# Exchange of keys and outputs from SBUF to SBUF, and a reordered front and border, in a linear-attention and FP4 network kernel

## What is computed

```
xn = layernorm(x)
# attention block, H = 8 heads, DK = DV = 128, chunks of 128 tokens
h  = rmsnorm(xn) * attn_norm_w
q, k, v = h @ Wq, h @ Wk, h @ Wv                      # 256 -> 1024 each
per head, chunk after chunk, state S (128 x 128):
    o = tril(q k^T) v + q S ;  S = S + k^T v
o  = rmsnorm(o) * out_norm_w                          # per head
x2 = xn + o @ Wo
s  = x2 + (silu(h2 @ Wgate) * (h2 @ Wup)) @ Wdown     # h2 = rmsnorm(x2) * mlp_norm_w, 1024 wide
# second network on xn, activations and weights rounded to FP4 in blocks of 16
g  = silu(fp4_linear(silu(gate4) * up4, w_down))      # 704 wide
out = x + s * g
```

## Time and profile before

| | before |
|---|---|
| median of 3 runs | 1065.65 us (1065.02 to 1065.74) |
| the profiled execution | 1065.84 us, its span 1064.1 us |
| PE busy | 1052.4 us, 99% |
| DVE busy | 904.9 us, 85% |
| ACT busy | 526.8 us, 50% |
| granted TensorE clock | 1.00 |
| q1 (SP's DMAs) | 141.88 MB, 43.1% of 16 engines |

### The profile page before, as it was taken

One profiled execution on the slowest core, in us unless ns is written; L12 is line 12 of the kernel. 1 busy time (PEld: TensorE's weight loads), 2 busy tenths in 40 slices (PEclk: granted clock), 3 DMA queues, 4 the chain that ended last, 5 costly groups with the idle time before them and its releaser, 6 DMA issues.

```text
span 1064.1 us, 18735 instructions
## 1 busy us (share of the span) xinstructions
PE 1052.4 (99%) x6792; PEld 961.5 (90%) x6792; DVE 904.9 (85%) x1859; ACT 526.8 (50%) x1481; POOL 47.3 (4%) x68
## 2 busy tenths in 40 slices
PE   8999999999999999999999999999999999999998
PEld 6899999998999989999998889999999999999997
DVE  6788888888888888888887798888888889889887
ACT  6664655755656546557555634443333333243332
POOL 0000000000000000000000000101001010101010
PEclk9999999999999999999999999999999999999999
DMA  7455355455364553554545723253433233323213
GB/s 244 143 160 175 106 173 168 138 156 167 134 192 133 157 175 120 184 173 127 166 149 161 195 68 97 80 158 94 120 90 119 85 120 98 122 85 93 86 57 112
DMA packets 166219, 143.07 MB, mean 134 GB/s; under 512 B 28784, under 2 KB 162928, under 8 KB 166128
## 3 DMA queue, kind: packets, MB, share of 16 engines
q1 hardware_dynamic: 165440, 141.88, 43.1%
q10 hardware_dynamic: 688, 0.00, 0.0%
HBM read 77.27 MB, written 64.57 MB: 133 GB/s over the span
## 4 chain that ended last, share of the span: by engine, by line
PE 89%; DMA 4%; DVE 2%; SPq 2%; ACT 2%; issue 1%; POOL 0%; DVEq 0%; ACTq 0%; POOLq 0%
PE ps L261 69%; PE ps L712 5%; PE ps L756 5%; PE ps L750 4%; PE ps L736 4%; DMA moved<-work 3%; DMA r_gate<-moved 1%; SPq L410 1%; PE ps L838 1%; PE ps L639 1%; PE ps L599 1%; SPq L482 1%; DMA work<-kept_xq 1%; ACT work L945 0%; DVE work L1361 0%
## 5 line engine op out<-in xcount | busy, mean ns | idle before, releaser
L261 PE MATMUL ps<-r_k,r_gate_up 128*128 128x512 f32 x768 | 185.2, 391 | 0.5 <-DVE r_k L1544 0.5
L261 PEld LDWEIGHTS ps<-r_k,r_gate_up 128*128 128x128 f32 x768 | 141.5, 188 | 27.9 <-issue 0.7
L261 PE MATMUL ps<-r_o,onT 128*128 128x256 f32 x768 | 106.9, 288 | 0.4 <-DVE onT L1267 0.4
L261 PE MATMUL ps<-r_h,r_k 128*128 128x512 f32 (+1 forms) x393 | 105.2, 403 | 0.0
L261 PEld LDWEIGHTS ps<-r_q,r_v 128*128 128x128 f32 x768 | 99.7, 191 | 4.9 <-DVE r_v L1612 0.3
L261 PE MATMUL ps<-r_q,r_v 128*128 128x256 f32 x768 | 102.3, 283 | 0.0
L261 PE MATMUL ps<-r_h,r_q 128*128 128x512 f32 x384 | 98.1, 391 | 0.0
L945 ACT ACTIVATE work<-ps 128x128 f32<-128x128 f32 x256 | 67.1, 277 | 62.2 <-PE ps L756 62.1
L261 PE MATMUL ps<-r_v,r_h 128*128 128x512 f32 x384 | 97.4, 390 | 0.0
L261 PEld LDWEIGHTS ps<-r_o,onT 128*128 128x128 f32 x768 | 95.7, 190 | 0.8 <-DVE onT L1267 0.7
L921 ACT ACTIVATE work<-ps 128x512 f32<-128x512 f32 x64 | 38.3, 599 | 108.6 <-PE ps L261 108.6
(11 more groups left out here) (160 smaller groups left out, 1987.6 us busy)
## 6 DMA issues: line engine op xcount, KB each, us to landing
moved<-work SPq DMA_DIRECT2D x63, 512.0 KB, 2.9
r_gate<-moved SPq DMA_DIRECT2D x252, 128.0 KB, 2.5
kept_h<-work SPq DMA_DIRECT2D x31, 384.0 KB, 2.6
work<-kept_h SPq DMA_DIRECT2D x124, 96.0 KB, 2.3
work<-in_L_attn_hidden_states SPq DMA_DIRECT2D x15, 512.0 KB, 5.2
kept<-work SPq DMA_DIRECT2D x9, 514.0 KB, 4.3
kept_h<-work SPq DMA_DIRECT2D x9, 512.0 KB, 3.7
kept_xq<-work SPq DMA_DIRECT2D x8, 512.0 KB, 5.4
```

The lines of the kernel that those rows point to most:

```text
L261: done = pe.matmul(out_ap, a, b, start=first and n == 0, stop=last and n == 2, skip_group_check=skip)
```

## The change

- `exchange` has no tile in HBM. Four DMAs go from `leaving` to `arriving`, the q-th reading slot q of all 128 partitions and writing 32 partitions with four such slots each. They are issued when keys and outputs are ready in `leaving` and `arriving` has been read by both turns. `moved_out` is gone; who waited for it waits for `moved_in`, the landing of all four.
- A destination partition now holds four neighbouring source partitions and not four that are 32 apart, so both DVE turns write with "(d a)" in place of "(a d)": every fourth column of a row.
- ACT: `permute_k` comes before `copy_k` and both after one wait; the wait is for `moved_in`. PE's `turn_h` waits for `copy_k` in addition.
- DVE: `ln_roots` with `rms_factor` (h=1) and `x2_factor` (h=3) come before the turns and no longer behind them.
- Front: WARM 4 instead of 5; Wo is loaded after the first exchange, into another place, and split in two parts in steps 0 and 1 (ACT) and 1 and 2 (DVE); PE waits for weight parts 4, 5 and 6 each before its first use and not for all before step 0; ACT's order of weights and copies is changed; x of block 1 is loaded after the exchange.
- Border: the loads of `kept_xq` and `kept_w4` are issued in steps 11 and 12 of the last batch instead of both in 13; `xT_hi_of` on ACT comes in step 14 right behind `copy_k`; one product of the second network is put ahead of an output projection.

```diff
-                    sp.dma_start(moved.rearrange("b p x -> p b x"), leaving.rearrange("p b i x -> p b (i x)"))\
-                      .then_inc(moved_out, 16)
                     if again:
                         sp.wait_ge(k_tok_ready, value - 1)
                     if turned_o is not None:
                         sp.wait_ge(oT_ready, turned_o)
-                    sp.wait_ge(moved_out, 16 * value)
                     for q in range(QUADS):
-                        sp.dma_start(arriving[q * QUAD:(q + 1) * QUAD].rearrange("p a i x -> p a (i x)"),
-                                     moved[q].rearrange("(a p) x -> p a x", a=QUADS)).then_inc(moved_in, 16)
+                        sp.dma_start(arriving[q * QUAD:(q + 1) * QUAD].rearrange("p a i x -> p (a i x)"),
+                                     leaving[:, q, :, :].rearrange("p i x -> p (i x)")).then_inc(moved_in, 16)
...
-                    dve.transpose(k_tok.rearrange("p c (a d) -> p c a d", a=QUADS), k_landed).then_inc(k_tok_ready, 1)
+                    dve.transpose(k_tok.rearrange("p c (d a) -> p c a d", a=QUADS), k_landed).then_inc(k_tok_ready, 1)
...
-                    dve.transpose(oT.rearrange("p c (a d) -> p c a d", a=QUADS), o_landed).then_inc(oT_ready, 1)
+                    dve.transpose(oT.rearrange("p c (d a) -> p c a d", a=QUADS), o_landed).then_inc(oT_ready, 1)
...
-        WARM = 5
+        WARM = 4
...
-                for i, (n, c0, c1) in enumerate(w_parts):
...
+                for i in range(W_OUT):
+                    load_weight(i)
...
                 exchange(1, again=False)
+                sp.dma_start(raw_out, Wo.rearrange("(h p) n -> p h n", p=P)).then_inc(w_loaded[W_OUT], 16)
+                sp.wait_ge(xn_ready, 1)
+                sp.dma_start(x_in, x_blocks[1]).then_inc(x_loaded, 16)
...
-                pe.wait_ge(w_ready, W_OUT)
                 pe.wait_ge(q_ready, 1)
...
                         pe.wait_ge(k_perm_ready, t0 + j + 1)
+                        if (b, j) == (0, 0):
+                            pe.wait_ge(w_ready, 4)
                         project(wk, B_K, h_next, s_next, k_done)
+                        if (b, j) == (0, 0):
+                            pe.wait_ge(w_ready, 5)
                         project(wq, B_Q, h_next, s_next, q_done)
+                        if (b, j) == (0, 0):
+                            pe.wait_ge(w_ready, W_OUT)
...
                 weight_hi(2)
+                permute_k(1)
+                copy_k(1)
                 weight_hi(3)
-                copy_k(1)
-                permute_k()
-                for i in range(4, len(w_parts)):
-                    weight_hi(i)
                 copy_q(1, 0)
-                act.wait_ge(w_ready, 5)
-                for c in range(CH):
+                weight_hi(4)
+                act.wait_ge(w_ready, 4)
+                copy_v(1, 0, 0, FIRST_V_BANKS[0])
+                weight_hi(5)
+                for c in range(1, CH):
                     copy_v(c + 1, 0, c, FIRST_V_BANKS[c])
...
-                        copy_k(t0 + j + 2)
-                        if not (final and j == STEPS - LAG):
-                            act.wait_ge(moved_out, 16 * (t0 + j + 1))
-                            permute_k()
+                        if not (final and j == STEPS - LAG):
+                            act.wait_ge(moved_in, 16 * QUADS * (t0 + j + 1))
+                            permute_k(t0 + j + 2)
+                        copy_k(t0 + j + 2)
+                        if final and j == STEPS - LAG:
+                            xT_hi_of(0, range(KD))
...
+                    if first and j < 2:
+                        weight_out_hi(j)
...
+                    if n == 0 and h in (1, 2):
+                        weight_out_lo(h - 1)
...
+                    if h == 1 and ahead:
+                        ln_roots(1 - s, n + 1, mine)
+                        rms_factor(1 - s, mine)
+                    if h == 3:
+                        x2_factor(n + 1, mine)
                     if not (final and j == STEPS - 1):
                         turn_k(t0 + j + 1)
...
-                        dve.wait_ge(moved_out, 16 * (t0 + j + 2))
+                        dve.wait_ge(moved_in, 16 * QUADS * (t0 + j + 2))
...
                 gate_up4(0, 0, (0,), (1,))
+                gate_up4(0, 0, (1,), (0,))
                 out_projection(H - 2, batches * STEPS - 1)
-                gate_up4(0, 0, (1,))
+                gate_up4(0, 0, (1,), (1,))
```

More of the change, by code:

```diff
@@ L168, in build @@
         raw_w = [work[:, at:at + WCOLS].rearrange("p (k n) -> p k n", k=KD)
-                 for at in (v_at, v_at + WCOLS, not_yet)]
-        raw_w.append(work[:, not_yet + WCOLS:not_yet + 2 * WCOLS].rearrange("p (h n) -> p h n", h=H))
+                 for at in (v_at + WCOLS, v_at, not_yet)]
         stats = one.cut(CH, 6)
@@ L175, in build @@
         small = one.cut(12, CH)
+        out_at = one.at
         xq_new = one.cut(CH * D)
@@ L183, in build @@
         assert one.at - down4_at >= N4P and max(PIECE4) <= CH * D
+        assert one.at - out_at >= WCOLS
+        raw_out = work[:, out_at:out_at + WCOLS].rearrange("p (h n) -> p h n", h=H)
         leaving = one.cut(QUADS, 2, CH * QUAD)
@@ L278, in build @@
         FIRST = 2 * P
-        w_parts = [(1, 0, FIRST), (0, 0, FIRST), (2, 0, BANK), (1, FIRST, HD), (0, FIRST, HD), (2, BANK, HD), (3, 0, D)]
+        w_parts = [(1, 0, FIRST), (0, 0, FIRST), (2, 0, BANK), (1, FIRST, HD), (0, FIRST, HD), (2, BANK, HD)]
         W_OUT = 6
-        projections = ((Wq, wq), (Wk, wk), (Wv, wv), (Wo, wo))
-        w_loaded = [sem(f"weight_part{i}_loaded") for i in range(len(w_parts))]
+        projections = ((Wq, wq), (Wk, wk), (Wv, wv))
+        w_loaded = [sem(f"weight_part{i}_loaded") for i in range(len(w_parts) + 1)]
         w_hi, w_ready = sem("weight_hi_done"), sem("weight_ready")
@@ L456, in attention_transfers @@
                             sp.wait_ge(piece_ready, n)
+                        else:
+                            sp.wait_ge(w_ready, W_OUT + 2)
                         load_piece(n, range(QUADS // 2) if h == CH + 1 else range(QUADS // 2, QUADS))
@@ L760, in attend @@
                         if (j - LAG) % H == 0:
-                            pe.wait_ge(w_ready, len(w_parts))
                             pe.wait_ge(x2_summed, n0 + s + 1)
+                        if first and j - LAG in (0, CH):
+                            pe.wait_ge(w_ready, W_OUT + 1 + (j - LAG) // CH)
                         out_projection((j - LAG) % H, t0 + j - 1)
@@ L921, in copy_k, with permute_k @@
                     act.activation(kT, ps[:, B_K, :], ACT.Copy).then_inc(k_ready, 1)
-                def permute_k():
+                def permute_k(value):
+                    act.wait_ge(k_done, value)
                     act.activation(k_perm,
@@ L1009, in weight_hi, with weight_out_hi @@
                     act.wait_ge(w_loaded[i], 16)
-                    scale = nw_out[:, 0:1] if n == 3 else 1.0
-                    act.activation(projections[n][1][:, HI, :, c0:c1], raw_w[n][:, :, c0:c1], ACT.Copy, scale=scale)\
+                    act.activation(projections[n][1][:, HI, :, c0:c1], raw_w[n][:, :, c0:c1], ACT.Copy).then_inc(w_hi, 1)
+                def weight_out_hi(i):
+                    act.wait_ge(w_loaded[W_OUT], 16)
+                    heads = slice(i * CH, (i + 1) * CH)
+                    act.activation(wo[:, HI, heads, :], raw_out[:, heads, :], ACT.Copy, scale=nw_out[:, 0:1])\
                        .then_inc(w_hi, 1)
@@ L1086, in attention @@
                             weights4_hi(2 + k, raw_gate4[:, k, :])
-                        xT_hi_of(0, range(KD))
                     if final and last:
@@ L1372, in early_extras @@
                         fp4_grid(piece, grid_w, mine)
-                    if h == 1 and ahead:
-                        ln_roots(1 - s, n + 1, mine)
-                        rms_factor(1 - s, mine)
                     if h == 2 and n:
                         residual(1 - s, n)
-                    if h == 3:
-                        x2_factor(n + 1, mine)
                     if h == 3 and rounds_piece:
@@ L1498, in attention @@
                             turn_o()
-                    if first and j == 0:
-                        weight_lo(W_OUT)
-                        dve.wait_ge(w_ready, len(w_parts))
                     early_extras(b, j, mine)
```

36 lines of the change are left out of this document (19 added, 17 removed).

## The result

The changed kernel takes 1083.44 us (median of 4 runs, 1082.53 to 1084.62) beside 1065.7 for the kernel before (4 runs, 1065.02 to 1066.6): a ratio of 1.0166, 95% interval 1.0153 to 1.0178. It is 17.7 us slower where 8.3 us faster was forecast, and outside the range. The mechanism is that of rival A, at about two thirds of the price that it gave a turn (the rows are 0.38 to 0.40 us longer, not 0.57). The profiled execution took 1083.64 us, its span 1081.9, at a granted clock of 1.00 as before.

A forecast was written before the change was run, and what follows sets the result against it. PE, busy 99%, bounds the kernel; only its stalls, about 10 us, can be won. Exchange -4.8, order +1.5, front -2.6, border -0.8, -1.2 and -0.4 sum to -8.3: 1057.4 us from 1065.84; 8-in-10 range, leaving out slower turns, 1054 to 1067.

The forecast's parts named there:

- rival A: DVE turns write at half rate, 0.57 us more each; about 30 us reaches PE, 1095 us in all; chance 0.20.
- The strided turn: Both DVE turns writing every fourth column: cost of nothing chosen, bounded above by 0.57 us a turn, 1.14 a step.
- The decision point: Extra DVE turn time deciding the sign: from 0.26 us per turn, 0.5 a step costs 8 us, cancelling the gains.
- The exchange: Single hop replacing two in the middle steps: data lands earlier, DVE's wait for it goes, -4.8 us.
- the eight late steps: Middle steps of 9.15 to 10.50 us against 8.90, DVE waiting for the second hop; together they lose 4.8 us.
- The order inside a step: Small DVE operations ahead of the turns: state adds 0.5 us late in three h=1 steps, +1.5; h=3 covered.
- the three steps named: h=1 steps of first halves, batches 2 to 4: DVE's state adds 0.5 us late in each, +1.5 together.
- The front: Start and steps 0 to 3: shorter warm run, Wo later; -2.2 - 0.9 + 0.55 = -2.6 us.
- The border: Last batch's late steps: step 12 -0.8, step 14 -1.2, step 15's mask in time -0.4 us.
- The second phase: No edit there: starts at about 597.5 rather than 605.8, its length unchanged.
- Rival B: Only the front pays; the four transfers land 6 us or more after issue, DVE's waits stay; 1063 us; chance 0.13.
- Rival C: Reordering takes the gain back: 0.5 us in all 15 h=1 and h=3 steps, +7.5, 1063.5 to 1065 us; chance 0.09.

## Why the prediction was wrong

The step that failed is "The strided turn": it chose a cost of nothing. The turns measured 0.38 to 0.40 us more by their rows, 0.31 by the distance of the starts, and taking this one term away gives back 23.1 us and turns the sign: with contiguous turns the change is 5.5 us faster than the kernel before. The reason given was that the turns and the masked copy all take 0.69 to 0.73 us, so that "the engine handles one column at a time, whatever it reads". But all of those operations read and wrote runs of at least 32 neighbouring columns: the rows varied the arithmetic and not the stride, and could not speak on it. For reads, too, the sentence is wrong: DVE's low part took 1.07 instead of 0.68 when it read columns 128 B apart. The bounds of 0 and 0.57 us did hold the measured cost, and "No row of this trace has an operation of size that writes so" was the sentence to go by.

Rival A, given 0.20, is what happened, but its sum does not stand by its own terms. It took 0.57 a turn and set against it DVE's mean idle time, 0.65 us a step, which left 30 us. With the measured 0.39 the same sum leaves 0.13 a step, 8 us, and with 0.31 nothing; measured are 15.3 in the kernel before and 15.1 in the contiguous one. The price was too high and the cover, taken as a mean, too generous: steps of h=4 have next to none. The same account made step by step, set down before the run with strided turns in the kernel before, gave 16 us. The decision point (0.26 us a turn, 0.5 a step, costs 8 us) is borne out: one strided turn, 0.38 a step, costs 4.7 and two, 0.78 a step, cost 15.1, and on the line between them 0.5 comes to about 8.

Step by step:

- **The exchange**: -4.8 forecast, -4.4 (the single hop alone) to -4.5 measured over steps 3 to 58, with contiguous turns and the old order; the wait of the earlier trace rows is gone and the eight late steps are at 8.91 to 9.1. The landing was mis-sized: 3.2 to 3.4 us, and 0.60 for each of the three issues before it, against the 2.5 of the earlier trace rows and 1.3 for the three. The forecast had the data in 8 us after the scores and the norm into `leaving` 10 us after them. In the h=4 step of the contiguous kernel with the old order the issue starts 3.8 into the step, three issues and the landing make 5.3, so 9.1, and the norm comes at 10.2: a slack of 1.1 and not 2, which strided turns and the small operations used up. The norm waited 4 times in that kernel, 9 times with the stride, 13 with the order and 19 with both.
- **The order inside a step**: +1.5 forecast. With contiguous turns the three steps named grow by 0.4 each (9.29 to 9.32), near the 0.5 worked out, but the order costs 4.6 in all, since second halves, steps 0 to 2 and the last steps pay too; "in h=3 PE's extra turn covers it" held there. With strided turns it is 12.5: h=1 takes 10.03 to 10.04, not 9.4, and h=3 pays as well. So the term was too small by 3.1 even with contiguous turns, which is the distance from the forecast to the 1060.4 measured so; and it was sized alone, while it was not independent of the choice above.
- **The front**: -2.6 forecast. Scores of step 0 start at 19.03 and of step 1 at 26.53 (19.0 and 26.5 forecast; 21.17 and 29.60 before). What came back afterwards was 2.5 in steps 1 and 2 alone, not 0.55; in the contiguous kernel with the old order the net is -3.6 up to step 3.
- **The border**: -2.4 forecast. The steps 11 to 14 of the last batch changed by +1.6 after, and by -1.6 with contiguous turns and the old order; step 15, in which -0.4 was forecast, took 0.6 less in both. So the border as a whole is about +1 after and -2.2 with contiguous turns and the old order, near the forecast. Of that, 1.5 comes with the single hop alone. Step 12 took 8.94 instead of getting shorter (8.43 before), and step 14 took 9.26 (9.0 forecast, 10.19 before).
- **The second phase** moved as it is.
- Rival B is excluded by the single hop alone (-7.4 by its ratio). Rival C names a mechanism that is real (the order, 4.6 to 12.5 us), but with contiguous turns the change still gains 5.5 over the kernel before in the same runs.

Had the turns cost nothing, the change would have come to 1060.4, and with the small operations left where they were to 1055.8; the forecast of 1057.4 lies between, since the order was priced too low. Not settled: how the 15 to 23 us split between DVE's own length and the loop through the transfers, since both make the same steps late. The strided read was not tried on the side of PE's operands.

## What to carry to other kernels

Before an access pattern is priced at nothing, look whether any row of the trace has that pattern; rows with other arithmetic and the same stride say nothing on it, and then the sign of the forecast must not rest on it. Here a step of two float32 (8 B) cost nothing where a step of four (16 B) did, so a permutation with a step of four could be split: the writer takes steps of two, and the readers take pairs. And where two edits lengthen the same chain, price them together: here 15.1 and 4.6 us apart were 27.6 together.

## What the hardware showed unexpectedly

- A DVE turn of 128x512 float32 writing columns 4, 8, 16 and 32 B apart takes 0.70, 0.70, 1.08 and 1.12 us: a step between 8 and 16 B, with little slope behind it. The distances of the starts say the same: 0.59 to 0.62 up to 8 B, 0.91 to 0.93 at 16, 0.95 at 32.
- Reading 128 B apart costs DVE the same (0.68 to 1.07 us for 512 columns) and ACT more (0.63 to 1.16).
- A transfer of 128 KB from SBUF to SBUF lands 3.2 to 3.4 us after its issue and takes 0.60 to issue, against 2.5 and 0.43 from HBM to the same 32 partitions (medians); 64 KB land in 2.1 at the same issue time. I had not expected a single transfer to get slower without HBM; how much of it is the source and how much the other access pattern, no run separates. Two hops with a wait between them are still longer than one.
